# A Fourier cross-attention with a gated feed-forward layer: packed transforms, partition blocks exchanged by DMA, normalisations and exponentials on ScalarE

## The reference

```python
x = x + jnp.tanh(g_xattn[0]) * _L0_xattn_ref(_layernorm(x, axis=-1), ctx_4096, ctx_4096)
x = x + jnp.tanh(g_ffn[0]) * _L0_ffn_ref(_layernorm(x, axis=-1), L0_ffn_W_gate, L0_ffn_W_up, L0_ffn_W_down)
```

```python
qf = jnp.fft.fft(q, axis=2)
kf = jnp.fft.fft(k, axis=2)
corr = jnp.fft.ifft(qf * jnp.conj(kf), axis=2).real
topk = int(C * np.log(L))                      # 8
w, idx = jax.lax.top_k(corr.transpose(0, 1, 3, 2), topk)
w = jax.nn.softmax(w, axis=-1)
for i in range(topk):
    g = jnp.minimum(idx[:, :, None, :, i] + pos, L - 1)
    out = out + w[:, :, None, :, i] * jnp.take_along_axis(v, g, axis=2)
```

## Time and profile before

| | |
|---|---|
| median of 3 executions | 226.29 us |
| the profiled execution: device time | 226.31 us |
| its span, first to last instruction | 224.5 us |
| mean granted clock of PE | 0.992 of full speed |
| busy: PE, DVE, POOL, ACT | 96%, 67%, 60%, 44% of the span |

### The profile page before, as it was taken

How to read it: one execution, slowest core, us unless ns; L and a number is a source line. 1 busy time by engine, 2 the same in 40 slices (tenths; PEclk the granted TensorE clock), 3 DMA queues, 4 the chain that set the end, 5 groups by cost and what they waited for, 6 DMA issues and landing times.

```text
span 224.5 us, 6750 instructions
## 1 busy us (share of the span) xinstructions
PE 215.6 (96%) x2787; PEld 149.6 (67%) x2787; DVE 149.8 (67%) x424; ACT 98.4 (44%) x191; POOL 134.2 (60%) x148
## 2 busy tenths in 40 slices
...
GB/s 172 279 449 427 386 164 50 0 4 50 47 4 41 33 9 64 50 3 25 26 47 26 121 0 26 70 3 51 0 96 23 26 0 3 70 26 50 0 3 47
DMA packets 19885, 16.68 MB, mean 74 GB/s; under 512 B 15888, under 2 KB 16272, under 8 KB 19472
## 3 DMA queue, kind: packets, MB, share of 16 engines
...
## 4 chain that ended last, share of the span: by engine, by line
PE 89%; DVE 4%; DMA 2%; POOL 1%; issue 1%; SPq 1%; ACT 0%; DVEq 0%
PE psum L825 46%; PE psum L990 22%; PE psum L808 11%; PE psum L941 4%; DMA x_sb<-x 2%; PE psum L838 1%; DVE xn L769 1%; POOL prod_lo L512 1%; DVE prod L675 1%; PE psum L877 1%; PE psum L908 1%; PE psum L889 1%; PE psum L926 1%; DVE raw_stats L644 1%; PE psum L891 1%
## 5 line engine op out<-in xcount | busy, mean ns | idle before, releaser
L825 PE MATMUL psum<-xt_hi,wg 128*128 128x128 f16 (+1 forms) x504 | 54.9, 215 | 0.0
L825 PE MATMUL psum<-xt_lo,wg 128*128 128x128 f16 (+1 forms) x504 | 54.8, 215 | 0.0
L825 PE MATMUL psum<-xt_hi,wu 128*128 128x128 f16 (+1 forms) x504 | 54.0, 213 | 0.0
L825 PE MATMUL psum<-xt_lo,wu 128*128 128x128 f16 (+1 forms) x504 | 53.9, 213 | 0.0
L825 PEld LDWEIGHTS psum<-xt_hi,wg 128*128 128x128 f16 x504 | 45.8, 99 | 5.8 <-issue 3.8
L550 POOL TENSOR_TENSOR hid_lo<-hid,hid_hi 128x512 f16<-128x512 f32 (+2 forms) x32 | 33.5, 1051 | 26.7 <-ACT hid_hi L635 26.6
L825 PEld LDWEIGHTS psum<-xt_hi,wu 128*128 128x128 f16 x504 | 44.7, 98 | 5.2 <-issue 4.7
L825 PEld LDWEIGHTS psum<-xt_lo,wg 128*128 128x128 f16 x504 | 46.1, 99 | 0.6
L825 PEld LDWEIGHTS psum<-xt_lo,wu 128*128 128x128 f16 x504 | 45.0, 98 | 0.5
L990 PE MATMUL psum<-wd,hid_hi 128*128 128x512 f16 x112 | 42.5, 379 | 0.0
L990 PE MATMUL psum<-wd,hid_lo 128*128 128x512 f16 x112 | 42.4, 379 | 0.0
...
## 6 DMA issues: line engine op xcount, KB each, us to landing
out<-x_sb SPq DMA_DIRECT2D x8, 256.0 KB, 2.3
wg<-w_gate SPq DMA_DIRECT2D x1, 1792.0 KB, 11.2
wu<-w_up SPq DMA_DIRECT2D x1, 1792.0 KB, 14.9
wd<-w_down SPq DMA_DIRECT2D x1, 1792.0 KB, 19.0
ctx_sb<-ctx SPq DMA_DIRECT2D x1, 1024.0 KB, 21.0
x_sb<-x SPq DMA_DIRECT2D x1, 1024.0 KB, 22.8
x_sb<-x SPq DMA_DIRECT2D x2, 256.0 KB, 3.9
ctx_sb<-ctx SPq DMA_DIRECT2D x2, 256.0 KB, 4.4
```

Of the source, the lines that this page charges most:

```text
L825: last = nc.tensor.matmul(psum[:, bank, a * n:(a + 1) * n], w[:, k, m * P:(m + 1) * P], xt[:, e, k, tok], start=(k == 0 and part == 0), st ...
```

## The change

There are new matrices. For pairs 1 to 7 the context goes through one transform (`"values"`: its even and its odd frequencies, one under the other in the 128 output partitions) in place of two, and so do the weights (`"weights"`); the step `vspec` and part 1 of `wspec` remain for pair 0 alone. The products need the same numbers in other partitions as well. Those are now brought there by DMAs in a new step `turn` on SP: part 0 fills the upper half of `k_spec` with two transfers of 32 partitions, part 1 fills `v_turned` with four transfers of 31 or 32 partitions and one row of the context from memory. `prod` waits for part 0, and part 0 of `turn` waits for `vcopy`. The copies out of PSUM are two instructions over both banks in place of four. Both normalisations move from DVE to ACT as `x * rstd + shift`, and POOL computes `shift` with one more small instruction each time. `exp` of pairs 1 to 7 reads the correlation from PSUM in eight ACT instructions with a bias; DVE then only negates the largest value, and `match` waits for `exp`. The loads of pairs 2 and 3 are split, and those of pair 3 stand behind `w_up`. `ORDER` is a new list, with 1 and 10 warm matmuls in the second and third place in place of 4 and 9.

```diff
-FORWARD = ("even_kv", "even", "odd_v", "odd")
+FORWARD = ("query", "values", "weights")
...
-EXP_FROM_PSUM = ()
+EXP_FROM_PSUM = (1, 2, 3, 4, 5, 6, 7)
...
-WARM_UP = ((12, 4), (4, 7), (9, 7))
+WARM_UP = ((12, 4), (1, 7), (10, 7))
...
-            load(ctx_sb, cv, 2, 4, ctx_loaded[2])
-            load(x_sb, xv, 2, 4, x_loaded[2])
+            load(ctx_sb, cv, 2, 3, ctx_loaded[2])
+            load(x_sb, xv, 2, 3, x_loaded[2])
             sp.dma_start(wg[:, :, :], w_gate).then_inc(gate_loaded, 16)
             sp.dma_start(wu[:, :, :], w_up).then_inc(up_loaded, 16)
+            load(ctx_sb, cv, 3, 4, ctx_loaded[3])
+            load(x_sb, xv, 3, 4, x_loaded[3])
             sp.dma_start(wd[:, :, :], w_down).then_inc(down_loaded, 16)
-            load(ctx_sb, cv, 4, PAIRS, ctx_loaded[3])
-            load(x_sb, xv, 4, PAIRS, x_loaded[3])
+            load(ctx_sb, cv, 4, PAIRS, ctx_loaded[4])
+            load(x_sb, xv, 4, PAIRS, x_loaded[4])
             for step, p, n in order:
                 e = p % 2
+                if step == "turn":
+                    if n == 0:
+                        sp.wait_ge(v_copied, copies(p))
+                        if p == 2:
+                            sp.wait_ge(mixed_done, 4)
+                        if p >= 2:
+                            sp.wait_ge(prod_done, 2 * p - 2)
+                        for to, first in ((64, 32), (96, 0)):
+                            sp.dma_start(k_spec[to:to + 32, e, :, :], v_spec[first:first + 32, e, :, :])\
+                              .then_inc(k_moved[e], 16)
+                    else:
+                        if p > 2:
+                            sp.wait_ge(mixed_done, 4 * p - 4)
+                        for to, first, count in ((1, 33, 31), (32, 0, 32), (64, 96, 32), (96, 64, 32)):
+                            sp.dma_start(v_turned[to:to + count, e, :, :], v_spec[first:first + count, e, :, :])\
+                              .then_inc(v_moved[e], 16)
+                        sp.dma_start(v_turned[0:1, e, :, :], last_rows[p:p + 1, :, :]).then_inc(v_moved[e], 16)
...
+                pool.wait_ge(rstd_done, count)
+                nc.gpsimd.tensor_scalar(shift[tok, n:n + 1], mean, rstd[tok, n:n + 1], -1.0, ALU.mult,
+                                        ALU.mult).then_inc(shift_done, 1)
...
+            def normalise(to, p, tok, n, normed_done):
+                nc.scalar.activation(to, x_sb[tok, p, :], ACT.Identity, bias=shift[tok, n:n + 1],
+                                     scale=rstd[tok, n:n + 1]).then_inc(normed_done, 1)
...
+                if step == "vcopy" and p > 0:
                     act.wait_ge(k_spectra, p + 1)
...
+                    nc.scalar.activation(v_spec[:, e, :, :], psum[:, k_bank(p, 0):k_bank(p, 1) + 1, :], ACT.Copy,
+                                         scale=SPEC).then_inc(v_copied, 1)
+                if step == "kcopy" and p > 0:
...
+                    nc.scalar.activation(k_spec[0:L, e, :, :], psum[0:L, k_bank(p, 0):k_bank(p, 1) + 1, :], ACT.Copy,
+                                         scale=SPEC).then_inc(k_copied, 1)
...
                 if step == "prod":
                     dve.wait_ge(q_spectra, p + 1)
-                    dve.wait_ge(k_copied, 2 * p + n + 1)
+                    if p == 0:
+                        dve.wait_ge(k_copied, n + 1)
+                    else:
+                        dve.wait_ge(k_copied, copies(p))
+                        dve.wait_ge(k_moved[e], nth_turned(p, 2))
...
 ORDER = """
...
+match:0 exp:0 q_lo:1 vcopy:1 max:0.1 sum:0 kcopy:1 turn:1 scale:0 sub:0.1 wt:0 qspec:1 stats1:2 w_hi:0 gates:0
+wspec:0 rstd1:2 turn:1.1 prod:1 wspec:0.1 prod:1.1 p_hi:1 mix_prod:0 p_hi:1.1 p_lo:1 match:0.1 exp:0.1 mix:0
+k_hi:2 p_lo:1.1 mix_prod:0.2 q_norm:2 sum:0.1 k_lo:2 q_hi:2 lags:1 scale:0.1 scales:0 wt:0.1 max:1 q_lo:2
+mix:0.1 w_hi:0.1 sub:1 wspec:0.2 residual:0 exp:1 wspec:0.3 mix_prod:0.1 rstd2:0 k_hi:3 match:1 mix:0.2 k_lo:3
+xn:0 xt:0 mix_prod:0.3 kspec:2 x_hi:0 sum:1 mix:0.3 vcopy:2 x_lo:0 scale:1 stats1:3 gate:0 kcopy:2 turn:2
+residual:0.1 rstd1:3 w_rows_hi:1 w_t:1 qspec:2 w_rows_lo:1 tanh:0 q_norm:3 up:0 turn:2.1 prod:2 rstd2:0.1
+q_hi:3 silu:0 p_hi:2 prod:2.1 gate:0.1 xn:0.1 p_lo:2 w_t:1.1 hid:0 p_hi:2.1 q_lo:3 stats1:4 xt:0.1 tanh:0.1
```

More of the change, by code:

```diff
@@ L95, in parts @@
         return high, (m - high).astype(np.float16)
[L97 removed]
+    for n, m in enumerate((query, values, weights)):
         for part, v in enumerate(parts(m)):
@@ L112 @@
 ORDER = """
[L113 to L162, removed]
@@ L163 @@
-up:6.1 rstd2:7 tanh:6.1 silu:6.1 h_lo:6 gate:6.2 hid:6.1 xn:7 h_hi:6.1 up:6.2 x_rows_hi:7 tanh:6.2 x_t:7
-x_rows_lo:7 store:5 silu:6.2 gate:6.3 h_lo:6.1 hid:6.2 up:6.3 tanh:6.3 h_hi:6.2 silu:6.3 x_t:7.1 down:6
-hid:6.3 h_lo:6.2 h_hi:6.3 h_lo:6.3 down:6.1 gate:7 down:6.2 tanh:7 silu:7 down:6.3 up:7 out:6 store:6 gate:7.1
+warm:0 stats1:0 rstd1:0 kspec:0 q_norm:0 qspec:0 kcopy:0 stats1:1 kcopy:0.1 vspec:0 prod:0 rstd1:1 k_hi:1
+prod:0.1 lags:0 vcopy:0 k_lo:1 vcopy:0.1 lags:0.1 warm:0.1 max:0 q_norm:1 sub:0 kspec:1 warm:0.2 q_hi:1
@@ new lines @@
+residual:0.1 rstd1:3 w_rows_hi:1 w_t:1 qspec:2 w_rows_lo:1 tanh:0 q_norm:3 up:0 turn:2.1 prod:2 rstd2:0.1
+q_hi:3 silu:0 p_hi:2 prod:2.1 gate:0.1 xn:0.1 p_lo:2 w_t:1.1 hid:0 p_hi:2.1 q_lo:3 stats1:4 xt:0.1 tanh:0.1
+up:0.1 x_hi:0.1 silu:0.1 h_hi:0 p_lo:2.1 x_lo:0.1 wspec:1 hid:0.1 h_lo:0 h_hi:0.1 lags:2 mix_prod:1 gate:0.2
+mix_prod:1.1 rstd1:4 m_hi:1 max:2 m_hi:1.1 m_lo:1 up:0.2 sub:2 mix_prod:1.2 exp:2 m_lo:1.1 mix_prod:1.3
+gate:0.3 h_lo:0.1 m_hi:1.2 match:2 tanh:0.2 m_lo:1.2 m_hi:1.3 sum:2 kspec:3 tanh:0.3 m_lo:1.3 q_norm:4 mix:1
@@ new lines @@
+silu:0.2 vcopy:3 mix:1.1 scale:2 hid:0.2 mix:1.2 up:0.3 turn:3 h_hi:0.2 residual:1 w_rows_hi:2 h_lo:0.2
+kcopy:3 w_t:2 rstd2:1 qspec:3 down:0 w_rows_lo:2 xn:1 prod:3 silu:0.3 p_hi:3 w_t:2.1 stats1:5 x_rows_hi:1
+p_lo:3 down:0.1 x_t:1 prod:3.1 x_rows_lo:1 hid:0.3 p_hi:3.1 k_hi:4 p_lo:3.1 h_hi:0.3 wspec:2 q_hi:4 x_t:1.1
+mix_prod:2 h_lo:0.3 lags:3 mix_prod:2.1 m_hi:2 rstd1:5 down:0.2 max:3 m_hi:2.1 k_lo:4 down:0.3 sub:3
+mix_prod:2.2 exp:3 m_lo:2 mix_prod:2.3 gate:1 out:0 m_lo:2.1 m_hi:2.2 match:3 store:0 up:1 m_hi:2.3 turn:3.1
```

279 lines of the change are left out of this document (166 added, 113 removed).

## The result

The changed kernel takes 257.51 us (255.6 to 258.7, 4 executions) against 226.21 us: ratio 1.1367, 95% interval 1.1309 to 1.1424. I had forecast slower, 232.0, with a range of 217 to 238. The direction is right, the size is not: 31 us were lost, not 6. (Ratios here leave disturbed executions out, medians hold them all, so the two can differ by a little.)

The account below looks back on a forecast made before the run. DVE and dependences of pairs 0 and 1 bound the start, PE's work the rest. Span 224.5, landmark 15.7 later, PE work 10.0 less, rest 0: 230.2, plus 1.8 around the span gives 232.0 us, range 217 to 238.

Parts of the forecast that it names:

- The work on PE: Fourteen transforms of 0.72 us each go, so PE work behind the landmark falls by 10.0 us.
- the landmark: First `gate` of pair 0, at 28.98 us before, forecast at 44.7; what comes after it counts as PE work.
- My first rival: Exchange of pair 1 isn't held up by the loads: landmark at 30.8, 218.1 us in all; chance 0.20.
- The exchange behind the bulk loads: In SP's queue, `turn` of pair 1 lands behind all loads at 32.4 us (bounds 18.5 and 34), delaying `prod:1`.
- From `prod:1` to the landmark: Path at the start, mostly DVE: 12.3 us against 10.3 before, bounds 10.3 and 14.
- What it adds, off the path: Added ACT and POOL work and longer bank 4 path mostly hidden behind PE: sum 0, ends -2 and +4 us.
- the second rival: One DMA engine handles the 31-partition transfer in 4.9 us, delaying close transposes up to 2.4 us each: 239; chance 0.09.

Follow-up runs that it names:

- e12_no_turn: The changed kernel with the whole step `turn` and every wait for it left out, so attention of pairs 1 to 7 is wrong: 217.9 us, ratio 0.9640.
- e3_both: The changed kernel with loads from `w_up` on held until after part 0 of `turn` of pair 1, and the 31-partition transfer split: 228.6 us, ratio 1.0024.
- e2_split31: The changed kernel with the transfer of 31 partitions issued as one of 16 and one of 15: 242.0 us, ratio 1.0672.
- e5_order: e3_both with part 1 of `turn` of pairs 2, 5, 6 moved behind low transposes of pairs 1, 3, 4: 225.4 us, ratio 0.9903.
- e9_pair0_first: e5_order with loads of pairs 5 to 7 after pair 1's transposes, and `prod` of pairs 1, 2 behind pair 0 steps: 225.4 us, ratio 0.9958.

## Why the prediction was wrong

The work on PE: right. Ten us were to go, 9.8 went behind the landmark, and the span without exchange is 215.6 against 224.5, 8.9 less. My first rival (218.1) comes within 0.2 us of `e12_no_turn` (217.9), but that is partly luck: its landmark was to be at 30.8 and came at 28.5, and the time behind it was to be 185.5 and is 187.1. Nor does its condition describe a complete kernel: `e3_both`, with the exchange no longer held up and the landmark at 31.2, takes 228.6.

The exchange behind the bulk loads: right in mechanism and place, 1.7 us short (34.1 for 32.4). I treated SP's issues as free; behind the loads one took 8.2 us.

From `prod:1` to the landmark: 14.1 us for 12.3, just over the upper bound. I had noted that PE's low clock falls there and gave it no price; the stretch from 30 to 40 us ran at 0.50, and PE lost 3 us of speed between `prod:1` and 42 us (5.9 us of work at half the clock). How much of that lay in the path isn't shown.

The step that failed is the one headed "What it adds, off the path", with the sum of all later waits set at 0 and +4 as its end, and the second rival kept out of it with a chance of 0.09. The waits behind the landmark came to +16.3 and their clock to +6.3. The forecast was 25.5 us short, 232.0 for 257.5, and these two terms are 22.6 of it. The row that could have told was there: 2.5 us of slack between a transpose's landing and its `gate`. I gave each close transpose 2.4 us, 7.2 in all, and named the right pairs (1, 3, 4), but weighed it as unlikely because no row showed such a shape, counted only the time of the transfer and not SP's 3.5 us for the issues of `turn` in front of the transpose, left out pair 6, and again left out the clock. `e2_split31` against the changed kernel prices the transfer of 31 partitions at 15.5 us, clock included. What is left of the two terms are the waits that `e2_split31` still has behind the landmark (3.0, 1.7, 1.3, 1.1, 0.6 and 0.5 us) and their clock; SP's issues in front of the transposes have a part in these that wasn't measured alone. The Trainium skill states the rule ("DMA: Bandwidth & Descriptors", section "Why a DMA increments its semaphore by 16 and not by 1"), and these runs agree with it: one of the 16 engines was at work in front of the transpose that PE waited for (share 0.07), and 16 with 15 partitions take its median landing from 4.1 back to 2.4 us.

What stays open: why no complete version came near 218. `e3_both`, `e5_order` and `e9_pair0_first` show a lower mean clock than `e12_no_turn` (0.976 to 0.985 against 1.00 in the profiles) and waits of 1 to 4 us between 17 and 60 us. For `e3_both` part 1 holds 7 of the 10.7 us, as said; how much of the last 7 us, from 225 to 218, is the landing time of the exchanges of pairs 1 and 2, how much SP's issues and how much the clock after such waits, wasn't separated.
